# Two attention passes of a macaron block on one core: the same work in another order on ScalarE, VectorE and GpSimd, and in the second pass the next slot's first scores moved between two output products on TensorE

## What is computed

```python
q = _rms_norm(x @ wq_a.T, q_norm_w) @ wq_b.T            # 32 heads, 128 + 64 (rotated) columns
kv = x @ wkv_a.T                                         # latent 128, rotated key 64
kv_up = _rms_norm(kv_c, kv_norm_w) @ wkv_b.T
scores = (jnp.einsum('bshd,bthd->bhst', q_nope, k_nope) + jnp.einsum('bshd,btd->bhst', q_pe, k_pe)) * scale
scores = jnp.where(causal[None, None], scores, jnp.finfo(scores.dtype).min)
probs = jax.nn.softmax(scores, axis=-1)
out = jnp.einsum('bhst,bthd->bshd', probs, v).reshape(b, s, NH * V_DIM)
return out @ wo.T
```

## Time and profile before

| what | value |
|---|---|
| median of 3 runs | 2350.86 us |
| profiled execution, own time | 2356.33 us |
| its span | 2354.5 us |
| granted TensorE clock, mean | 0.989 |
| PE busy | 2181.5 us (93%) |
| DVE busy | 1611.1 us (68%) |
| ACT busy | 1371.7 us (58%) |
| POOL busy | 1257.2 us (53%) |
| DMA, mean over the span | 110 GB/s |

### The profile page before, as it was taken

One profiled execution on the slowest core, in us unless ns is written; L12 is line 12 of the kernel. 1 busy time (PEld: TensorE's weight loads), 2 busy tenths in 40 slices (PEclk: granted clock), 3 DMA queues, 4 the chain that ended last, 5 costly groups with the idle time before them and its releaser, 6 DMA issues.

```text
span 2354.5 us, 44541 instructions
## 1 busy us (share of the span) xinstructions
PE 2181.5 (93%) x11548; PEld 1815.1 (77%) x11548; DVE 1611.1 (68%) x3415; ACT 1371.7 (58%) x3561; POOL 1257.2 (53%) x1643
## 2 busy tenths in 40 slices
PE   8979999999999999999889979999999999999988
PEld 7957777777777777777778957888888888887877
DVE  7646667666766666767777646666666666666677
ACT  6545566656665566665666545555555555555553
POOL 5325565666656656566554345555555555555543
PEclk9989999999999999999999989999999999999999
DMA  4024433333344343433424133333333333333321
GB/s 164 14 60 127 135 130 131 114 99 88 126 135 130 126 135 128 133 110 118 159 97 142 28 110 107 106 106 106 106 106 106 106 106 106 106 106 107 104 92 72
DMA packets 217104, 258.01 MB, mean 110 GB/s; under 512 B 145616, under 2 KB 174416, under 8 KB 214992
## 3 DMA queue, kind: packets, MB, share of 16 engines
q1 hardware_dynamic: 212432, 244.64, 33.6%
q10 hardware_dynamic: 4608, 12.58, 1.6%
HBM read 127.14 MB, written 79.69 MB: 88 GB/s over the span
## 4 chain that ended last, share of the span: by engine, by line
PE 52%; DVE 12%; DMA 11%; issue 8%; ACT 7%; POOL 7%; SPq 3%; POOLq 0%; DVEq 0%; ACTq 0%
PE ps L861 39%; DMA stage<-in_wo 8%; PE ps L940 4%; DVE xacc L2184 4%; DVE arena L1837 3%; ACT arena L1383 3%; PE ps L1224 2%; PE ps L1168 2%; DMA arena<-arena 2%; PE ps L887 1%; SPq L756 1%; DVE negmax L2163 1%; DVE ps L2161 1%; ACT stage L1683 1%; PE ps L875 1%
## 5 line engine op out<-in xcount | busy, mean ns | idle before, releaser
L2184 DVE TENSOR_TENSOR xacc<-ps,xacc 128x512 f32<-128x512 f32 x896 | 602.8, 686 | 280.8 <-PE ps L861 267.4
L1837 DVE TENSOR_TENSOR arena<-ps,arena 128x512 fp32r<-128x512 f32 (+4 forms) x744 | 428.8, 578 | 326.3 <-ACT arena L1383 325.3
L861 PE MATMUL ps<-arena,extra 128*128 128x512 f32 x1920 | 540.0, 410 | 70.4 <-DVE xacc L2184 67.6
L861 PEld LDWEIGHTS ps<-arena,extra 128*128 128x128 f32 x1920 | 338.2, 188 | 190.1 <-DVE xacc L2184 114.9
L1683 ACT ACTIVATE stage<-ps,negmax 128x128 f32<-128x128 f32 (+6 forms) x512 | 261.3, 510 | 381.3 <-DVE negmax L2163 376.4
L861 PE MATMUL ps<-zT,arena 128*128 128x512 f32 (+1 forms) x1746 | 451.1, 403 | 10.3 <-ACT stage L1383 7.0
L1383 ACT ACTIVATE arena<-ps 128x512 fp32r<-128x512 f32 (+4 forms) x744 | 360.0, 506 | 115.4 <-PE ps L861 50.4
L2468 POOL TENSOR_TENSOR extra<-extra_plain,extra 128x256 fp32r<-128x256 f32 (+1 forms) x256 | 224.9, 879 | 320.4 <-ACT extra L1383 319.7
L861 PEld LDWEIGHTS ps<-zT,arena 128*128 128x128 f32 x1746 | 320.1, 191 | 80.6 <-ACT stage L1383 10.6
L861 PE MATMUL ps<-arena 128*128 128x512 f32 x960 | 262.6, 410 | 30.5 <-POOL arena L2468 24.3
L1692 ACT ACTIVATE stage<-stage,rrec 128x128 f32<-128x128 f32 (+6 forms) x512 | 235.8, 532 | 71.0 <-DVE rrec L2169 71.0
(11 more groups left out here) (129 smaller groups left out, 3159.2 us busy)
## 6 DMA issues: line engine op xcount, KB each, us to landing
kept_b<-arena SPq DMA_DIRECT2D x16, 3584.0 KB, 11.0
arena<-kept_b SPq DMA_DIRECT2D x112, 512.0 KB, 5.6
arena<-arena SPq DMA_DIRECT2D x128, 128.0 KB, 3.0
stage<-in_wo SPq DMA_DIRECT2D x16, 1024.0 KB, 13.1
stage<-stage SPq DMA_DIRECT2D x248, 64.0 KB, 2.0
extra<-arena SPq DMA_DIRECT2D x120, 128.0 KB, 3.0
kept_q<-arena SPq DMA_DIRECT2D x16, 768.0 KB, 4.1
arena<-kept_q ACTq DMA_DIRECT2D x32, 384.0 KB, 6.2
```

The costliest lines, as they stand in the source:

```text
L861: last = nc.tensor.matmul(dst, w, m, start=start and n == 0, stop=stop and n == len(passes) - 1, skip_group_check=skip)
L1837: return nc.vector.tensor_tensor(dst, src, part.bitcast(F32), ALU.subtract)
L2184: nc.vector.tensor_tensor(xs, bank_y(k, j), xs, ALU.add).then_inc(y_added, 1)
```

## The change

The waits and the work are the same; orders change. On PE, in the second attention (`p` = 1), slots 0 and 2 issue the next slot's `scores(k + 1, 0)` between output products 3 and 4, and slots 1 and 3 leave it out at their start. VectorE follows with `maxima(k + 1, 0)` between additions 5 and 6. On ScalarE, VectorE and GpSimd the orders within most slots change, in a way of its own for slots 1 and 2 of the first attention and for slots 0 and 2 of the second.

```diff
@@ TensorE, slot
-                scores(p, g, k, 0, False, last)
+                if not (p and k % 2):
+                    scores(p, g, k, 0, False, last)
                 scores(p, g, k, 1, False, last)
...
                 out_(2, 3)
                 fills(p, g, k, "first", ev)
+                if p and k % 2 == 0:
+                    scores(p, g, k + 1, 0, False, last)
                 out_(4, 5)
                 values(n, before, False)
@@ ScalarE, body
-                    if k % 2 == 0:
+                    if k == 2 and p == 0:
                         turned(n, before, 0)
+                        split_a(m, 1)
+                        turned(n, before, 1)
                         exps(p, g, k, 0)
-                        turned(n, before, 1)
+                        split_a(m, 2)
+                        fills(k, "output")
+                        split_b(g, T3, last)
+                        turned(n, before, 2)
                         exps(p, g, k, 1)
-                    else:
+                        split_b(g, T4, last)
+                        turned(n, before, 3)
+                        exps(p, g, k, 2)
+                        split_b(g, B22, last)
+                        exps(p, g, k, 3)
+                    elif k == 1 and p == 0:
...
+                        turned(n, before, 2)
+                        split_a(m, 2)
+                        turned(n, before, 3)
+                        exps(p, g, k, 2)
+                        fills(k, "second")
                         split_b(g, B11, last)
-                    exps(p, g, k, 3)
...
+                        norms(p, g, k, 0, 3)
+                        valued(n, whole=False)
+                        norms(p, g, k, 3)
+                        split_a(n, 0)
+                        continue
+                    elif k % 2 == 0 and p:
+                        turned(n, before, 0)
+                        exps(p, g, k, 0)
+                        turned(n, before, 1)
+                        split_a(m, 1)
+                        exps(p, g, k, 1)
+                        fills(k, "output")
+                        turned(n, before, 2)
+                        split_a(m, 2)
+                        turned(n, before, 3)
+                        exps(p, g, k, 2)
+                        exps(p, g, k, 3)
@@ VectorE, slot
-                maxima(p, g, k, 0)
+                b22 = k == 2 and p == 0
+                if not (p and k % 2):
+                    maxima(p, g, k, 0)
                 if k % 2:
                     maxima(p, g, k, 1)
-                fills("front")
-                pt_split(n, before, 0)
-                pt_split(n, before, 1)
-                if k % 2 == 0:
+                    fills("front")
+                    pt_split(n, before, 0)
+                    pt_split(n, before, 1)
+                elif b22:
+                    pt_split(n, before, 0)
+                    pt_split(n, before, 1)
                     maxima(p, g, k, 1)
+                else:
+                    pt_split(n, before, 0)
+                    maxima(p, g, k, 1)
+                    pt_split(n, before, 1)
...
-                pt_split(n, before, 3)
-                fills("second")
-                maxima(p, g, k, 3)
-                adds(2, 3)
+                if b22:
+                    pt_split(n, before, 3)
+                    adds(2, 3)
+                    maxima(p, g, k, 3)
+                elif k % 2 == 0 and p:
+                    adds(2, 3)
+                    pt_split(n, before, 3)
+                    maxima(p, g, k, 3)
+                else:
+                    pt_split(n, before, 3)
+                    fills("second")
+                    maxima(p, g, k, 3)
+                    adds(2, 3)
...
+                adds(4)
                 if k == 1 and p == 0:
                     second_row(g, ev, False)
-                adds(4)
                 fills("first")
-                adds(5, 6)
+                adds(5)
+                if p and k % 2 == 0:
+                    maxima(p, g, k + 1, 0)
+                adds(6)
@@ GpSimd, sums (all_first is set for slot 2 of the first attention)
-                split(0)
+                if not all_first:
+                    split(0)
                 G.tensor_tensor(s3, a22, a21, ALU.subtract).then_inc(o_sum, 1)
+                if all_first:
+                    split(0)
                 split(1)
```

More of the change, by code:

```diff
@@ L1685, in exps, with norms @@
                                      accum_out=rowsum[:, k % 2, i:i + 1]).then_inc(exp_done, 1)
-            def norms(p, g, k):
+            def norms(p, g, k, first=0, end=NS):
                 n, u = slot_n(p, g, k), k % 2
                 act.wait_ge(rec_ready, n + 1)
-                for i in range(NS):
+                for i in range(first, end):
                     pr = prob[u][:, poff(u, i):poff(u, i) + keys_of(u, i)]
@@ L1707, in valued @@
                        by_head(bank_pv[:, a * 2 * P:(a + 1) * 2 * P])).then_inc(o_raw, 1)
-                split_a(n, 0)
+                if whole:
+                    split_a(n, 0)
             def split_a(n, group):
@@ L1745, in body @@
                         turned(n, before, 1)
-                    split_a(m, 1)
-                    fills(k, "output")
-                    if k == 1 and not last:
-                        split_wpe(p, g + 1)
-                    turned(n, before, 2)
-                    turned(n, before, 3)
-                    exps(p, g, k, 2)
-                    split_a(m, 2)
-                    if k == 2 and p == 0:
-                        split_b(g, T3, last)
-                        split_b(g, T4, last)
-                    fills(k, "second")
-                    if k == 1 and p == 0:
+                        split_a(m, 1)
+                        fills(k, "output")
+                        if not last:
+                            split_wpe(p, g + 1)
+                        turned(n, before, 2)
[3 more added lines that the diff above has]
+                        fills(k, "second")
                         split_b(g, B11, last)
-                    exps(p, g, k, 3)
-                    if k == 2 and p == 0:
-                        split_b(g, B22, last)
-                    if k == 1 and p == 0:
+                        exps(p, g, k, 3)
                         split_b(g, T2, last)
@@ L1766, in body @@
                         fills(k, "first")
+                        norms(p, g, k, 0, 3)
+                        valued(n, whole=False)
+                        norms(p, g, k, 3)
+                        split_a(n, 0)
+                        continue
[3 more added lines that the diff above has]
+                        turned(n, before, 1)
+                        split_a(m, 1)
+                        exps(p, g, k, 1)
+                        fills(k, "output")
+                        turned(n, before, 2)
+                        split_a(m, 2)
+                        turned(n, before, 3)
+                        exps(p, g, k, 2)
+                        exps(p, g, k, 3)
+                    else:
+                        if k % 2:
+                            exps(p, g, k, 0)
+                            turned(n, before, 0)
+                            exps(p, g, k, 1)
+                            turned(n, before, 1)
+                        else:
+                            turned(n, before, 0)
+                            exps(p, g, k, 0)
+                            turned(n, before, 1)
+                            exps(p, g, k, 1)
+                        split_a(m, 1)
+                        fills(k, "output")
+                        if k == 1 and not last:
+                            split_wpe(p, g + 1)
+                        turned(n, before, 2)
+                        turned(n, before, 3)
+                        exps(p, g, k, 2)
+                        split_a(m, 2)
+                        fills(k, "second")
+                        exps(p, g, k, 3)
                     norms(p, g, k)
-                    if k == 1 and p == 0:
-                        valued(n)
-                        continue
                     fills(k, "first")
```

8 lines of the change are left out of this document (5 added, 3 removed).

## The result

| | before | changed |
|---|---|---|
| median of 4 runs, us | 2352.35 (2349.46 to 2356.67) | 2231.43 (2229.02 to 2234.47) |
| span of the profiled execution, us | 2354.5 | 2231.3 |

The ratio of the changed kernel to the one before is 0.9485 [0.9464, 0.9506]: 121 us less, where 98 were predicted.

The account below looks back on a forecast made before the run. PE, late for DVE's additions, bounds the second attention; a loop through the output-weights load bounds the first. Gains 48 + 49 + 1 = 98 us take 2356.33 to 2258, with the median 5.5 lower 2253; range 2238 to 2297.

Parts of the forecast that it names:

- (a): Second attention, slots 0 and 2: DVE makes additions 0 to 3 in a row; with (b) removes 1.22 us a slot.
- (c): Same slots as (a): `maxima` 1 goes ahead of `pt_split` 1, addition 0 comes 0.6 us earlier, lateness of 0.39 + 0.11 goes.
- (b): Same slots as (a): five score matmuls, 0.73 us, fill the place between products 3 and 4.
- Rival 2: Second attention: POOL's operand for slots 1 and 3 becomes the wait; gain 24 us instead of 48, time 2277; chance 0.10.
- POOL starts about 0.6 earlier: First attention, end of slot 1: ACT evacuates the values before the last of four scalings, so POOL starts 0.6 us earlier.
- about 1.1: First attention, end of slot 1: of product 6's 1.2 us wait for addition 4, about 1.1 goes.
- The first attention's two waits: Slot 2: POOL's waits of 1.38 and 1.53 us for ACT before remainders of groups 1 and 2 go, 2.91 us.
- Rival 1: First attention: the rotation doesn't end earlier, so at most 10 us are gained there; time 2293; chance 0.14.
- Rival 3: Slower: in slot 2 of the first attention POOL's lateness holds up ACT's strict order; time above 2358; chance 0.03.
- Rival 4: Whole kernel: no measurable change, as all moved work finds the next wait at the same place; chance 0.05.
- PE's own limit: First attention: upper bound of the loop's gain, 4.3 us in each of 14 bodies, 60 us.
- the 0.48: First attention: the rotation's first operation took 1.75 us beside 1.27 for the last; 0.48 more if that goes.

Follow-up runs that it names:

- experiment 2: Kernel before with only ScalarE's and VectorE's new orders in slots 0 and 2 of the second attention, TensorE's order as before: 2315.86 us, ratio 0.9828.
- experiment 1: Kernel before with only the next slot's first scores moved between products 3 and 4 in the second attention, maxima moved to match: 2330.68 us, ratio 0.9888.
- experiment 11: Changed kernel with `split_a` 2 back behind exponential 2 in slots 0 and 2 of the second attention: 2237.69 us, ratio 0.9502.
- exp. 10: Kernel before with only `split_a` 2 ahead of `turned` 3 and exponential 2 in slot 1 of the first attention: 2349.08 us, ratio 0.9973.
- exp. 5: Changed kernel with `split_a` 2 back behind exponential 2 in slot 1 of the first attention: 2243.7 us, ratio 0.9517.
- exp. 6: Changed kernel with all four scalings again ahead of the evacuation of the values, slot 1 of the first attention: 2236.67 us, ratio 0.9493.
- exp. 7: Changed kernel with addition 4 back behind `second_row` in slot 1 of the first attention: 2248.65 us, ratio 0.9544.
- exp. 8: Changed kernel with ScalarE's order and the place of s3 on GpSimd as before in slot 2 of the first attention: 2281.83 us, ratio 0.9681.
- experiment 4: Changed kernel with the load of the next output weights issued just before the 3.5 MB copy of the kept weights: 2281.53 us, ratio 0.9676.
- experiment 9: Changed kernel with the kept-weights copy and the next output-weights load issued ahead of the stacking of `pe0`, first attention: 2233.53 us, ratio 0.9482.

## Why the prediction was right in direction and 23 us short

**What bounds it: right.** The second attention lay on PE and the first on the loop through the load of the output weights; after the change the chain runs over the same places, and PE still waits at `m0` for the load (4.1 us in ten waits), as the last list of the prediction said.

**Second attention: right, just above its ceiling.** Predicted 1.6 a slot and 48 us, at most 1.72 and 52; measured 3.51 a body, 1.76 a slot, 52.7 us. (The lower bound was worked out as 1.22 a slot and then taken as 1.15.) Of the three edits, (a) and (c) bring 1.27 a slot (experiment 2) and (b) 0.74 (experiment 1), with 0.25 in common. The prediction allowed for a small rest of lateness that does not exist. The margin of POOL's operand in slots 1 and 3 was put at 0.4. These are POOL's operand and PE's first use of it in the changed kernel:

```profile
1827.30 0.74 POOL L2530 TENSOR_TENSOR arena<-arena_plain,arena 128x256 fp32r<-128x256 f32 x1 [0.34 <-POOL extra_plain L2544]
...
1828.86 1.62 PE L861 MATMUL ps<-arena 128*128 128x512 f32 x6
```

It is ready at 1828.04 and wanted at 1828.86: 0.8. Without the moved copy 7 us are lost in all (experiment 11), 0.2 a slot, where the prediction had 0.5: with a margin twice as large, most of it stayed hidden. Rival 2 was named at the right place and did not come about.

**The step that failed: the size of the term "POOL starts about 0.6 earlier".** It measured 1.39. The runs divide the loop into its stages. All are means in us over four or five bodies between 680 and 1000; the two stages that are not shown, from the load to `m0` and from the rotation's end to the next load, stay within 0.1.

| kernel | `m0` to POOL's start in slot 2 | from there to the rotation | rotation | a body |
|---|---|---|---|---|
| before | 27.09 | 10.47 | 7.87 | 65.46 |
| before, `split_a` 2 moved (exp. 10) | 26.32 | 10.82 | 7.86 | 65.12 |
| changed | 25.71 | 7.30 | 7.69 | 60.76 |
| `split_a` 2 back (exp. 5) | 26.46 | 7.30 | 7.63 | 61.45 |
| evacuation back (exp. 6) | 26.33 | 7.30 | 7.63 | 61.31 |
| addition 4 back (exp. 7) | 25.71 | 8.28 | 7.79 | 61.80 |
| slot 2 back (exp. 8) | 25.71 | 10.86 | 7.47 | 64.10 |

The prediction took its 0.6 from one edit, the evacuation ahead of the last scaling, and that edit is worth what was said: 0.62 in this stage. Two other edits act on the loop and were booked at nothing there:
- *`split_a` 2 earlier in slot 1* is worth 0.75 in this stage, and with the 0.62 that is the whole 1.38. The prediction looked at DVE's remainder of 1.76 us as something that could meet the rotation, and not as a stretch that the change would take away. The inverses, the scalings and the evacuation are queued behind it (experiment 5).
- *Addition 4 ahead of `second_row`* is worth 1.07 a body (experiment 7), and none of it is in POOL's start: it lies in the next stage. The prediction booked its "about 1.1" to PE alone and then had the loop decide without it. But PE's product 6 stands ahead of `pe0`, ACT reads `pe0` ahead of the copy of T3, and POOL needs that copy before the rotation.

**The first attention's two waits: the size came out by luck in part.** 2.91 predicted, 3.15 measured between POOL's start and the rotation, and both waits are gone, as said. But with addition 4 back only 2.2 of it is left (8.28 against 10.47), although the two waits are gone there too: POOL then waits 0.68 for the copy of T3. The prediction warned of T4's copy only and gave no term for either. The 2.91 was met because addition 4 had moved. Rivals 1, 3 and 4 fall: the rotation does end earlier, and the exponentials that moved back delay nothing.

In whole bodies the four undone edits add up to 0.66 + 0.54 + 1.07 + 3.36 = 5.6 us where the whole is 4.7. In POOL's start they do add up; the surplus is in the stage behind it, where ACT's order and addition 4 hide each other's waits. VectorE's new order in slots 0 and 2 of the first attention was undone in no run, so what it is worth isn't shown.

**The bound "PE's own limit", 4.3: wrong.** It had PE able to do "about 61", with 0.7 lost again at scores 2. The loop is 60.77 with PE busy 59.89 in it, because busy time as the profile models it contained waiting, as the prediction itself remarked (61.32 before and 59.89 after for the same 308 matmuls at a granted clock of 1.00), and the 0.7 is not there. In the changed kernel exponential 0 is done at 845.90 (ACT's 845.65 and 0.25) and PE reaches scores 2 at 846.42 with no idle time. At 4.7 instead of 4.3 the lower end of the main case would have been 2232 and not 2238, still a little above the 2231.43 measured.

**The rule on the shared port.** The prediction said that by the rule of the Trainium skill (SBUF — State Buffer, "Who interferes with whom") the remainder of B22 would meet the rotation at another operation, so that the 0.48 would not come back in full. The rows agree. The rotation's first operation takes 1.27 now and its third, at 853.80, takes 1.59 where it took 1.29 before; this row of DVE starts 0.26 ahead of the third:

```profile
853.54 0.69 DVE L1879 TENSOR_TENSOR arena<-stage,arena 128x512 fp32r<-128x512 f32 x1
```

So 0.19 came back in all.

**Ends.** 3.0 us against 1. The loop's 67.6 also hold 1.9 us of the thirteenth body (6.55 less, where the others gave 4.69), which before was that much longer than the others. Its trace shows two things there: addition 4 stands behind three more operations of DVE, so PE waits 2.6 us for it at once and not 1.2, and right behind that wait the granted clock falls: 0.50 from 1090 to 1092, which is the lower of its two levels (1.2 of 2.4 GHz), and 0.83 as the mean from 1088 to 1098. In the changed kernel no wait of PE in that body is above 0.5 and its clock is 1.00. The prediction had taken all bodies as alike.

## What to carry to other kernels

When a loop goes through several in-order engines, walk the queue back on each of them and book every edit that stands ahead of one of the loop's steps, one that frees another engine from a wait too. An operation that takes 1.76 us where its twin takes 0.68 is a term of its own: ask what ran beside it, and whether the change moves the two apart. A stage that comes out at the predicted size is no proof either: here an edit that was booked elsewhere paid 1 us of it. Busy time of the bounding engine is a floor for a loop only as far as it holds no waiting, and moving a large copy or the load ahead of it only moved the last wait (experiments 4 and 9).

## What the runs showed of the hardware that I had not expected

- *A stretched pair.* A tensor operation of DVE with both inputs in SBUF that starts 0.09 to 0.11 us behind one of POOL ends after it and takes 1.74 to 1.76 us instead of 0.68, and POOL's next two take 2.98 to 2.99 instead of the 2.72 at the same place of the changed kernel. By the rule of the Trainium skill (SBUF — State Buffer, "Who interferes with whom") the two block each other; here the price, 1.1 us, lay on the loop.
- *Issuing stretches too.* Behind a copy of 3.5 MB and a load of 1 MB on SyncE, four transfers of 128 KB take 7.57 us to issue instead of 2.70, and 10.9 to land instead of 3.0 (experiment 9).
- *Going first doesn't mean going alone.* 1 MB issued just ahead of that copy takes 7.2 us instead of the 13.0 behind it, and the copy 15.2 instead of 11.0 (experiment 4).
- *One long wait, then a lower clock.* In the thirteenth body PE waits 2.57 to 2.59 us at once in the kernel before and in experiments 1 and 2, and in all three the granted clock falls at its end or just behind it; the mean of that body is 0.97, 0.97 and 0.95. With waits of at most 1.5 us in the same body (experiments 5, 7, 10 and the changed kernel) it is 1.00.
